# Two fused attention layers on one core: theta and phi split by GpSimd through the staging buffer, a fourth pair buffer, units in new slots, and the turned tile handled later

## The chip, the cores and the metric

The kernel runs on one core of a Trainium2 chip. The metric is the device time of one execution, in microseconds (us). The kernel before took 1897.72 us, the median of three runs (1893.85 to 1898.34). One execution was profiled; it took 1896.21 us, of which the trace spans 1894.4 us.

Engines are named as in the profile: PE is TensorE, DVE is VectorE, ACT is ScalarE, POOL is GpSimd, SP is SyncE, which here only issues transfers.

## The reference: what is computed

The input `x` has 32 images of 128 channels by 32x32 pixels. Each image goes through two attention layers over its 1024 pixels.

```python
# layer 0 (D = 64)
t = conv1x1(x, W_theta, b_theta); p = conv1x1(x, W_phi, b_phi)
f = softmax(einsum('ndq,ndk->nqk', t, p) / sqrt(D), axis=-1)
x = x + conv1x1(einsum('nqk,nck->ncq', f, x), W_fuse, b_fuse)
# layer 1
h = group_norm(x, gn_w, gn_b)
q, k, v = (conv1x1(h, w, b) for w, b in ((q_w, q_b), (k_w, k_b), (v_w, v_b)))
attn = softmax(einsum('bic,bcj->bij', q, k) * C ** -0.5, axis=-1)
y = x + conv1x1(einsum('bcj,bij->bci', v, attn), p_w, p_b)
```

## The kernel before

**Tiles and slots.** The scores of a layer are 1024x1024, cut into eight tiles of 128 queries by 1024 keys. One iteration of the loop has 16 slots: slots 0 to 7 are the tiles of layer 0 of one image, slots 8 to 15 those of layer 1 of the image before it. Every engine has its own program that runs over the slots (`body`), and the order in it is written out by hand; the engines meet through semaphores only. The loop runs over the 32 images; head and tail iterations do a part of it.

**What PE does in slot s:** the scores of tile s (L429), one small product called a unit (L491), the transposes of the tile before if that one is "turned" (L458), and a quarter of the value product of the group that began six slots or more ago (L467). A group is four tiles: 0 to 3, 4 to 7, 8 to 11 and 12 to 15. Its value product begins in slot 6, 10, 14 and 2 (of the next iteration) and takes four slots. Its first quarter waits for the transfers of the group, for the low half of the turned tile (`s_tlo`), for the values' split (`s_split`) and for the product before to have been taken out of its bank (`s_taken`).

**How a tile gets its exponentials turned.** After the scores, DVE takes the row maximum (L723), ACT the exponential (L622), and the result is kept as two 16-bit halves, hi and lo, that have to be transposed. Tiles 1 and 2 of a group ("crossed") have their hi half made by ACT in `pair` (L647) and their lo half by DVE (L740); tile 0 ("copied") goes to `e_copied`, with its hi half from ACT (L645) and its lo half from POOL (L875). The halves of these three are then transposed by a DMA from `pair` to `et` (L350), one 128x2048 transfer per tile. `pair` has three places, one for each position in a group, so a tile's hi half waits until the transfer of the same position one group earlier has landed (L643). Tile 3 ("turned") is transposed by PE (L464), then ACT writes its hi half (L632) and DVE its lo half (L734).

**SP's queue** holds all transfers, in program order. In each group it issues: the denominators' reciprocals to DRAM (`rden_dram`, L363), then, when they have landed, the same as a broadcast row back to all partitions (`rden_row`, L374), then the three transposes. Between them stand the next image's load (`xs`, L385, slot 1), the stores of the result (L395) and the copies of phi (L405). An instruction of this queue that waits holds up all that follow.

**Units.** `UNITS` (L50) gives the unit of each slot: group norm (`gn1`, `gn2`), values (`v`, `w`), keys, queries, theta with phi (`tp`), and `mx`, a bound on the values. All use one PSUM bank `m_ps`, so a unit waits until ACT has emptied the bank of the one before (`s_evac`). Values, keys and queries go from the bank to `stage` by ACT, which has two places; POOL splits them into hi and lo (`split_units`, L877). Theta and phi don't use the stage: ACT writes the hi halves (L579, L581) and DVE the lo halves (L810, L814), right from the bank to `theta2` and `phi2`; then one DMA per half of the pixels copies phi to the other 64 partitions (L405).

The scores of slot 0 wait for these copies (`s_phi`, L442).

## Time and profile before

| | |
|---|---|
| median of 3 runs | 1897.72 us |
| profiled execution | 1896.21 us |
| its span | 1894.4 us |
| mean granted clock of PE | 0.991 |
| PE busy | 1715.3 us, 91% |
| DVE and ACT busy | 1445.5 and 1445.6 us, 76% each |
| POOL busy | 1260.9 us, 67% |
| packets in the DMA queue, share of 16 engines | 74.8% |

In the profile's lines, L426 is line 426 of the kernel and `o_ps<-et,v_hi` is what an instruction writes and reads. In a group of instructions there follow the shapes, the count, then the busy time in us and the mean ns of one, then the idle time of the engine before them with what ended it. "SPq" is the sequencer of SP, whose lines are issues of transfers.

### The profile page before, as it was taken

The numbers are of one execution on the slowest core, as the hardware profiler recorded it, in microseconds if no ns is written. First come the engines' busy times: TensorE is split into PE (matmuls) and PEld (weight loads), VectorE is DVE, ScalarE is ACT, GpSimd is POOL, SyncE is SP. The second block draws the span as 40 slices with busy tenths as digits, with TensorE's granted clock in tenths as the row PEclk, the third lists the DMA queues.
The fourth block names the chain that finished last, engine by engine and source line by source line (L and its number), as shares of the span: only waits on it lengthen the run. The fifth ranks groups of instructions, "written<-read, shape, count | busy, mean of one in ns | idle before, by whom it ended". The sixth has DMA issues, their size and how long they took to land.

```text
span 1894.4 us, 34418 instructions
## 1 busy us (share of the span) xinstructions
PE 1715.3 (91%) x8970; PEld 1103.0 (58%) x8970; DVE 1445.5 (76%) x1669; ACT 1445.6 (76%) x2152; POOL 1260.9 (67%) x1321
## 2 busy tenths in 40 slices
PE   3799999999999999999999999999999999999986
PEld 2455565656566665556665566665656565556553
DVE  4577778788778777778787778788778877878754
ACT  3587778778778777878787878777878777878754
POOL 2467766667776667776666776666776666776653
PEclk9799999999999999999999999999999999999999
DMA  2587787877787777878877878877878777778764
GB/s 53 115 141 149 158 169 148 160 157 151 162 164 159 158 159 147 164 155 161 161 155 148 165 154 163 165 147 156 164 150 166 162 146 160 163 147 166 149 134 95
DMA packets 860086, 286.33 MB, mean 151 GB/s; under 512 B 822305, under 2 KB 823201, under 8 KB 860065
## 3 DMA queue, kind: packets, MB, share of 16 engines
q1 hardware_dynamic: 860064, 286.08, 74.8%
q8 instruction: 9, 0.15, 0.0%
q14 instruction: 13, 0.10, 0.0%
HBM read 50.86 MB, written 17.04 MB: 36 GB/s over the span
## 4 chain that ended last, share of the span: by engine, by line
issue 25%; DVE 17%; ACT 14%; DMA 13%; PE 11%; POOL 10%; SPq 7%; DVEq 1%; POOLq 0%; ACTq 0%
DMA et<-pair 9%; SPq L350 6%; DVE neg_max L723 6%; PE o_ps L426 6%; ACT s_ps L622 4%; DMA rden_dram<-rden 3%; ACT pair L647 3%; PE s_ps L426 3%; DVE pair L740 2%; DVE phi L814 2%; PE s_ps L464 2%; POOL y_sb L974 2%; DVE x L777 2%; DVE x_max L800 2%; ACT et L632 2%
## 5 line engine op out<-in xcount | busy, mean ns | idle before, releaser
L426 PE MATMUL o_ps<-et,v_hi 128*128 128x512 f16 x2048 | 696.9, 382 | 39.9 <-DVE x L777 27.3
L723 DVE TENSOR_REDUCE neg_max<-s_ps 128x1 f32<-128x1024 f32 x512 | 624.5, 1220 | 62.7 <-PE s_ps L426 52.2
L740 DVE SCALAR_TENSOR_TENSOR pair<-s_ps,pair 128x1024 f16<-128x1024 f32 x256 | 312.3, 1220 | 105.6 <-ACT pair L647 104.6
L426 PE MATMUL o_ps<-et,v_lo 128*128 128x512 f16 x1024 | 390.0, 381 | 0.0
L426 PEld LDWEIGHTS o_ps<-et,v_hi 128*128 128x128 f16 x2048 | 202.7, 99 | 283.6 <-issue 92.5
L426 PE MATMUL s_ps<-phi,theta 128*128 128x512 f32 x1024 | 330.8, 446 | 9.2 <-ACT e_copied L622 4.5
L622 ACT ACTIVATE s_ps<-s_ps,neg_max 128x1024 f32<-128x1024 f32 x256 | 277.2, 1083 | 60.4 <-DVE neg_max L723 59.7
L875 POOL TENSOR_TENSOR pair<-e_copied,pair 128x1024 f16<-128x1024 f32 x128 | 274.2, 2142 | 27.5 <-ACT pair L645 27.5
L964 POOL TENSOR_TENSOR x<-x,xr 128x512 f32<-128x512 f32 x64 | 81.1, 1267 | 283.4 <-DVE x L777 283.4
L734 DVE SCALAR_TENSOR_TENSOR et<-s_ps,et 128x1024 f16<-128x1024 f32 x128 | 156.7, 1224 | 146.4 <-ACT et L632 146.4
L647 ACT ACTIVATE pair<-s_ps 128x1024 f16<-128x1024 f32 x256 | 261.9, 1023 | 8.1
L426 PE MATMUL s_ps<-k_hi,q_hi 128*128 128x512 f32 x512 | 246.3, 481 | 7.9 <-POOL q_lo L875 2.3
L645 ACT ACTIVATE pair<-e_copied 128x1024 f16<-128x1024 f32 x128 | 135.3, 1057 | 150.5 <-DMA et<-pair 145.6
L426 PEld LDWEIGHTS s_ps<-phi,theta 128*128 128x128 f32 x1024 | 195.9, 192 | 70.4 <-ACT e_copied L622 6.2
L426 PE MATMUL s_ps<-k_hi,q_lo 128*128 128x512 f32 x512 | 202.1, 395 | 0.0
L426 PE MATMUL s_ps<-k_lo,q_hi 128*128 128x512 f32 x512 | 201.5, 393 | 0.0
L622 ACT ACTIVATE e<-s_ps,neg_max 128x1024 f32<-128x1024 f32 x128 | 142.5, 1114 | 47.1 <-DVE neg_max L723 45.3
L632 ACT ACTIVATE et<-s_ps 128x1024 f16<-128x1024 f32 x128 | 131.1, 1024 | 58.3 <-PE s_ps L464 56.2
L464 PE MATMUL s_ps<-ident_sb,e 128*128 128x128 f32 x1024 | 138.1, 278 | 32.4 <-ACT e L622 32.4
L875 POOL TENSOR_TENSOR v_lo<-stage,v_hi 128x512 f16<-128x512 f32 x128 | 148.5, 1160 | 10.7
L622 ACT ACTIVATE e_copied<-s_ps,neg_shifted 128x1024 f32<-128x1024 f32 x128 | 143.0, 1117 | 4.2
L464 PEld LDWEIGHTS s_ps<-ident_sb,e 128*128 128x128 f32 x1024 | 109.8, 141 | 61.8 <-ACT e L622 61.8
(131 smaller groups left out, 2885.1 us busy)
## 6 DMA issues: line engine op xcount, KB each, us to landing
rden_row<-rden_dram SPq DMA_DIRECT2D x128, 256.0 KB, 3.8
xs<-in_x SPq DMA_DIRECT2D x32, 512.0 KB, 3.9
phi<-phi SPq DMA_DIRECT2D x64, 256.0 KB, 3.1
out_y<-y_sb SPq DMA_DIRECT2D x64, 256.0 KB, 2.4
et<-pair SPq DMA_TRANSPOSE x384, 4.6
rden_dram<-rden SPq DMA_DIRECT2D x128, 2.0 KB, 1.5
w_f<-in_w_fuse_t SPq DMA_DIRECT2D x1, 64.0 KB, 2.2
ident_sb<-in_ident SPq DMA_DIRECT2D x1, 64.0 KB, 2.1
```

The costliest lines, as they stand in the source:

```text
L350: sp.dma_start_transpose(et[:, t // GROUP % 4, r, :, :], pair[:, r, :, :].rearrange("q a n -> q (a n)")).then_inc(s_pair_t[r], 16)
L426: mm = pe.matmul(out, lhs_t, rhs, start=start and n == 0, stop=stop and n == len(terms) - 1)
L464: mm = pe.transpose(s_ps[:, part(t), kb * P:(kb + 1) * P], e[:, kb * P:(kb + 1) * P], ident[:, :])
L622: nc.scalar.activation(to[:, :], s_ps[:, r, :], ACT.Exp, bias=bias, accum_out=den[:, g, t % GROUP:t % GROUP + 1]).then_inc(s_exp, 1)
L632: nc.scalar.activation(et[:, t // GROUP % 4, TURNED, 0:KB, :], s_ps[:, part(t), :].rearrange("k (b q) -> k b q", b=KB), ACT.Copy, scale=E_ ...
L645: nc.scalar.activation(pair[:, r, 0, :], e_copied[:, :], ACT.Copy).then_inc(s_copied_hi, 1)
L647: nc.scalar.activation(pair[:, r, 0, :], s_ps[:, part(t), :], ACT.Copy, scale=E_SCALE).then_inc(s_pair_hi, 1)
L723: nc.vector.tensor_reduce(neg_max[:, t % 4:t % 4 + 1], s_ps[:, part(t), :], AX.X, ALU.max, negate=True).then_inc(s_max, 1)
L734: nc.vector.scalar_tensor_tensor(out=blocks[:, KB:2 * KB, :], in0=s_ps[:, part(t), :].rearrange("k (b q) -> k b q", b=KB), scalar=E_SCALE, ...
L740: nc.vector.scalar_tensor_tensor(out=pair[:, r, 1, :], in0=s_ps[:, part(t), :], scalar=E_SCALE, in1=pair[:, r, 0, :], op0=ALU.mult, op1=AL ...
L875: nc.gpsimd.tensor_tensor(out, in_, hi, ALU.subtract).then_inc(sem, 1)
L964: nc.gpsimd.tensor_tensor(x1[:, cols], x1[:, cols], xr[:, cols], ALU.add).then_inc(s_x1, 1)
```

## The change

1. **Theta and phi through the stage.** ACT writes the unit `tp` as one 128x512 activation to `stage`. POOL makes hi and lo from it in a new buffer `tp_hl`. Four DMAs per half of the pixels bring them to `phi2` (two times hi and lo) and `theta2` (hi and lo). The four instructions of ACT and DVE per half go.
2. **Two parts of pair.** `PAIRS` is 4; the copied tile uses place 0 and place 3 in turn, so its hi half waits for the transfer of two groups ago.
3. **Units in new slots**, with a new table of stage places and of POOL's lags. `mx` moves from slot 14 to 9, `v0` from 15 to 14, `w0` and `w1` from 8 and 9 to 7 and 11, `q1` from 7 to 8. The copies stand in SP's slots 12 and 14, before in 11 and 13.
4. **The turned tile later.** PE runs the quarter of the value product before the transposes of the slot; ACT runs the exponential before the turned hi half; DVE makes the turned lo half one slot later, in the slot in which it also takes out a value product.
5. The units `tp`, `q`, `k` start with the two terms of the hi half and wait for the lo half before the third. The value product's first quarter waits only for the splits of the first half of the values, the third quarter for the rest.

```diff
-UNITS = {0: "gn1", 1: "gn2", 2: "v1", 4: "k0", 5: "k1", 6: "q0", 7: "q1", 8: "w0", 9: "w1", 10: "tp0", 12: "tp1",
-         14: "mx", 15: "v0"}
+UNITS = {0: "gn1", 1: "gn2", 2: "v1", 4: "k0", 5: "k1", 6: "q0", 7: "w0", 8: "q1", 9: "mx", 10: "tp0", 11: "w1",
+         12: "tp1", 14: "v0"}
-PAIRS = 3
+PAIRS = 4
-PHI_SLOTS = {11: "tp0", 13: "tp1"}
+TP_COPY_SLOTS = {12: "tp0", 14: "tp1"}
+    def place(s):
+        return PAIRS - 1 if s % GROUP == COPIED and s // GROUP % 2 else s % GROUP
...
-            def phi_copies(it, s):
+            def tp_copies(it, s):
...
-                sp.wait_ge(s_tp, before(tp_at, it, unit) + 1)
+                sp.wait_ge(s_split, before(staged_at, it, unit) + 1)
                 sp.sem_inc(s_carrier)
-                sp.dma_start(phi2[0:D, :, cols].bitcast(F32), phi2[D:C, :, cols].bitcast(F32)).then_inc(s_phi, 16)
+                sp.wait_ge(s_scores, before(tile_at, it, PHASE))
+                sp.sem_inc(s_carrier)
+                theta_hl, phi_hl = (tp_hl[half][rows, :, :].bitcast(F32) for rows in (slice(0, D), slice(D, C)))
+                sp.dma_start(phi2[0:D, :, cols].bitcast(F32), phi_hl).then_inc(s_tp_copy[half], 16)
+                sp.dma_start(phi2[D:C, :, cols].bitcast(F32), phi_hl).then_inc(s_tp_copy[half], 16)
+                sp.dma_start(theta2[0:D, cols].bitcast(F32), theta_hl[:, 0, :]).then_inc(s_tp_copy[half], 16)
+                sp.dma_start(theta2[D:C, cols].bitcast(F32), theta_hl[:, 1, :]).then_inc(s_tp_copy[half], 16)
...
                     if s == 0:
-                        pe.wait_ge(s_phi, 16 * before(tp_at, it, 0))
+                        for n in range(2):
+                            pe.wait_ge(s_tp_copy[n], 16 * TP_COPIES * before(mx_at, it, 0))
...
                     unit(it, s)
+                    values(it, s)
                     transposes(it, s)
-                    values(it, s)
...
-                if name[0] == "t":
-                    cols = slice(int(name[-1]) * HALF, (int(name[-1]) + 1) * HALF)
-                    act.wait_ge(s_scores, before(tile_at, it, PHASE))
-                    nc.scalar.activation(theta2[0:D, cols], m_ps[0:D, :], ACT.Identity,
-                                         bias=vec_ready[0:D, 0:1]).then_inc(s_theta, 1)
-                    nc.scalar.activation(phi2[D:C, 0, cols], m_ps[D:C, :], ACT.Identity,
-                                         bias=vec_ready[D:C, 0:1]).then_inc(s_evac, 1)
-                    return
+                elif name[0] == "t":
+                    nc.scalar.activation(to, m_ps[:, :], ACT.Identity, bias=vec_ready[:, 0:1]).then_inc(s_evac, 1)
...
                 for s in range(SLOTS):
+                    exponentials(it, s)
                     turned_hi(it, s)
-                    exponentials(it, s)
...
-            def take_lo(it, s):
-                t = s - 2
+            def turned_lo(it, s):
+                t = s - 3
...
                     take_bounds(it, s)
                     maxima(it, s)
+                    turned_lo(it, s)
                     normalised(it, s)
-                    take_lo(it, s)
-                    take_unit(it, s)
+                    pair_lo(it, s)
                     reciprocals(it, s)
+                    bound_to_scale(it, s)
...
                 pool.wait_ge(s_evac, before(taken_at, it, s) + 1)
-                if name[0] in "qk":
+                if name[0] == "t":
+                    pool.wait_ge(s_tp_copy[half], 16 * TP_COPIES * or_none(before(mx_at, it, s) - 1))
+                    hi, lo = tp_hl[half][:, 0, :], tp_hl[half][:, 1, :]
+                    hi_read = hi.bitcast(F32)
+                elif name[0] in "qk":
```

**SP's queue from slot 11 to slot 15, before.** The transfers in program order, in an iteration of the head in which all of them stand; `et<-pair` are the transposes of tiles 9, 8 and 10 and, at the end, of 13 and 12, `phi<-phi` the copies, `rden` the reciprocals.

```order
L350 DMA_TRANSPOSE et<-pair 128x16x128 [waits pair_ready,value_product_ready]
L350 DMA_TRANSPOSE et<-pair 128x16x128 [waits copied_pair_ready,value_product_ready]
L405 DMA phi<-phi 64x2x512 [waits theta_phi_ready]
L350 DMA_TRANSPOSE et<-pair 128x16x128 [waits pair_ready,value_product_ready]
L405 DMA phi<-phi 64x2x512 [waits theta_phi_ready]
L363 DMA rden_dram<-rden 128x4 [waits rden_ready,rden_row_loaded0]
L374 DMA rden_row<-rden_dram 128x512 [waits rden_in_dram0,value_product_taken]
L350 DMA_TRANSPOSE et<-pair 128x16x128 [waits pair_ready,value_product_ready]
L350 DMA_TRANSPOSE et<-pair 128x16x128 [waits copied_pair_ready,value_product_ready]
```

**The same stretch after.**

```order
L364 DMA_TRANSPOSE et<-pair 128x16x128 [waits pair_ready,value_product_ready]
L424 DMA phi<-tp_hl 64x2x512 [waits unit_split,scores_ready]
L425 DMA phi<-tp_hl 64x2x512
L426 DMA theta<-tp_hl 64x512
L427 DMA theta<-tp_hl 64x512
L378 DMA rden_dram<-rden 128x4 [waits rden_ready,rden_row_loaded0]
L424 DMA phi<-tp_hl 64x2x512 [waits unit_split,scores_ready]
L425 DMA phi<-tp_hl 64x2x512
L426 DMA theta<-tp_hl 64x512
L427 DMA theta<-tp_hl 64x512
L389 DMA rden_row<-rden_dram 128x512 [waits rden_in_dram0,value_product_taken]
L364 DMA_TRANSPOSE et<-pair 128x16x128 [waits pair_ready,value_product_ready]
```

The two copies, one before and one behind the transpose of tile 10 and both ahead of the reciprocals, have become eight: four behind that transpose and four between the reciprocals' way out and their way back, ahead of the transposes of tiles 13 and 12.

**DVE in slots 13 and 14, before.** `neg_max` is the maximum of a tile, `et<-s_ps,et` the turned lo half of tile 11, `x<-o_ps` the value product of tiles 4 to 7 taken out, `rden` its reciprocals' last step.

```order
L733 REGISTER_ALU
L734 SCALAR_TENSOR_TENSOR et<-s_ps,et 128x1024 [waits et_hi_ready]
L809 REGISTER_ALU
L810 SCALAR_TENSOR_TENSOR theta<-m_ps,vec_ready,theta 64x512 [waits theta_hi_ready]
L813 REGISTER_ALU
L814 SCALAR_TENSOR_TENSOR phi<-m_ps,vec_ready,phi 64x512 [waits unit_taken_by_act]
L722 REGISTER_ALU
L723 TENSOR_REDUCE neg_max<-s_ps 128x1 [waits scores_ready]
L777 TENSOR_TENSOR x<-o_ps,rden_row 128x512 [waits h_hi_ready,h_ready,x1_res_ready1,rden_row_loaded1,value_product_ready]
L752 SCALAR_TENSOR_TENSOR den_scaled<-den,v_scale,e_factors 128x4 [waits value_scale_ready1,exp_ready]
L756 ISA [waits den_scaled_ready]
L757 RECIPROCAL rden<-den_scaled 128x4 [waits rden_in_dram0]
```

**The same stretch after.**

```order
L749 REGISTER_ALU
L750 TENSOR_REDUCE neg_max<-s_ps 128x1 [waits scores_ready]
L757 REGISTER_ALU
L758 SCALAR_TENSOR_TENSOR et<-s_ps,et 128x1024 [waits et_hi_ready]
L806 TENSOR_TENSOR x<-o_ps,rden_row 128x512 [waits h_hi_ready,h_ready,x1_res_ready1,rden_row_loaded1,value_product_ready]
L781 SCALAR_TENSOR_TENSOR den_scaled<-den,v_scale,e_factors 128x4 [waits value_scale_ready1,exp_ready]
L785 ISA [waits den_scaled_ready]
L786 RECIPROCAL rden<-den_scaled 128x4 [waits rden_in_dram0]
```

The lo half of tile 11 now stands behind the maximum of tile 13, right ahead of the value product that PE waits for; the four instructions on theta and phi of each iteration are gone.

**PE in slot 0, behind the unit `gn1`, before.** `ident_sb,e` are the transposes of the turned tile 15, `o_ps` a quarter of the value product.

```order
L501 MATMUL m_ps<-mean_var,group_avg_sb 128x2 [waits mean_var_ready]
L462 ISA
L464 MATMUL s_ps<-ident_sb,e 128x128 [waits exp_ready]
L464 MATMUL s_ps<-ident_sb,e 128x128 x7
L426 MATMUL o_ps<-et,v_hi 128x512
L426 MATMUL o_ps<-et,v_lo 128x512
L426 MATMUL o_ps<-et,v_hi 128x512 x2
L426 MATMUL o_ps<-et,v_lo 128x512
L426 MATMUL o_ps<-et,v_hi 128x512
```

**The same stretch after.**

```order
L530 MATMUL m_ps<-mean_var,group_avg_sb 128x2 [waits mean_var_ready]
L511 ISA
L448 MATMUL o_ps<-et,v_hi 128x512 [waits unit_split]
L448 MATMUL o_ps<-et,v_lo 128x512
L448 MATMUL o_ps<-et,v_hi 128x512 x2
L448 MATMUL o_ps<-et,v_lo 128x512
L448 MATMUL o_ps<-et,v_hi 128x512
L485 ISA
L487 MATMUL s_ps<-ident_sb,e 128x128 [waits exp_ready]
L487 MATMUL s_ps<-ident_sb,e 128x128 x7
```

The transposes and the six matmuls of the value product have changed places.

## Rows read from the trace of the kernel before

**Rows 1.** The page: busy time, share of the span and instructions; then the DMA queue.
```profile
PE 1715.3 (91%) x8970; PEld 1103.0 (58%) x8970; DVE 1445.5 (76%) x1669; ACT 1445.6 (76%) x2152; POOL 1260.9 (67%) x1321
...
q1 hardware_dynamic: 860064, 286.08, 74.8%
```

**Rows 2.** Waits of the whole span: total us, times, longest us.
```profile
ACT pair L645 <- DMA et<-pair: 145.6, 83, 3.5
...
PE m_ps L426 <- ACT stage L591: 34.0, 30, 1.6
PE s_ps L464 <- ACT e L622: 32.4, 66, 1.4
...
PE o_ps L426 <- DVE x L777: 27.3, 30, 1.4
```

**Rows 3.** PE's timeline: start us, us, instruction.
```profile
156.25 0.38 PE L426 MATMUL o_ps<-et,v_hi 128*128 128x512 f16 x1
...
949.05 0.38 PE L426 MATMUL o_ps<-et,v_hi 128*128 128x512 f16 x1
...
974.78 0.39 PE L426 MATMUL o_ps<-et,v_hi 128*128 128x512 f16 x1
...
983.82 1.27 PE L426 MATMUL s_ps<-phi,theta 128*128 128x512 f32 x4
...
1006.15 0.38 PE L426 MATMUL o_ps<-et,v_hi 128*128 128x512 f16 x1
...
1741.52 0.38 PE L426 MATMUL o_ps<-et,v_hi 128*128 128x512 f16 x1
```

**Rows 4.** SP's timeline in the same iteration: start us, us of issue.
```profile
979.29 0.35 SPq L363 DMA_DIRECT2D rden_dram<-rden  x1
980.89 0.32 SPq L374 DMA_DIRECT2D rden_row<-rden_dram  x1
981.69 8.21 SPq L350 DMA_TRANSPOSE et<-pair  x3
990.38 0.36 SPq L385 DMA_DIRECT2D xs<-in_x  x1
...
1001.44 2.36 SPq L350 DMA_TRANSPOSE et<-pair  x1
```

**Rows 5.** The transpose issued at 1001.44: issue in ns, and from issue to landing.
```profile
L350 SPq DMA_TRANSPOSE et<-pair x1: 2364/2364/2364, 1001.4 to 1001.4; - x1
...
DMA to landing us min/median/max: 4.5/4.5/4.5
```

**Rows 6.** All copies of phi: issue ns min/median/max; from issue to landing.
```profile
L405 SPq DMA_DIRECT2D phi<-phi x64: 590/622/1195, 15.5 to 1769.6; - x64
...
DMA to landing us min/median/max: 3.0/3.1/5.2
```

**Rows 7.** Windows: us, busy of PE, PEld, DVE, ACT, POOL, clock, DMA share, GB/s.
```profile
978.00:978.50 0.50, 0.00 (x0) 0.00 (x0) 0.50 (x1) 0.50 (x1) 0.00 (x0) 1.00 0.84 180
978.50:979.00 0.50, 0.26 (x2) 0.17 (x3) 0.37 (x4) 0.47 (x3) 0.33 (x1) 1.00 1.00 197
979.00:979.50 0.50, 0.50 (x4) 0.24 (x3) 0.50 (x3) 0.50 (x1) 0.50 (x1) 1.00 0.72 148
979.50:982.00 2.50, 2.50 (x16) 2.00 (x14) 2.34 (x5) 1.84 (x4) 2.50 (x2) 1.00 0.03 1
```

**Rows 8.** Groups of instructions, three of DVE and one of PE (L508 is mx).
```profile
L723 DVE TENSOR_REDUCE neg_max<-s_ps 128x1 f32<-128x1024 f32 x512 | 624.5, 1220 | 62.7 <-PE s_ps L426 52.2 <-issue 8.0
...
L734 DVE SCALAR_TENSOR_TENSOR et<-s_ps,et 128x1024 f16<-128x1024 f32 x128 | 156.7, 1224 | 146.4 <-ACT et L632 146.4
...
L777 DVE TENSOR_TENSOR x<-o_ps,rden_row 128x512 f32<-128x512 f32 x64 | 68.0, 1062 | 33.1 <-PE o_ps L426 32.1
...
L508 PE MATMUL m_ps<-w_f_abs,x_max_row 128*128 128x128 f32 x64 | 12.6, 279 | 2.4 <-ACT phi L581 2.4
```

**Rows 9.** The start of the program, PE's timeline: the first scores.
```profile
34.33 3.78 PE L426 MATMUL s_ps<-phi,theta 128*128 128x512 f32 x8 [3.74 <-DVE bound L687]
```

More of the change, by code:

```diff
@@ L162, in until_part_before, with until_stage_before, last @@
         return value(lambda i: count(kind, 0, (part_before(i, s) or 0) + 1), it)
+    def until_stage_before(it, s):
+        def last(i):
+            g = SLOTS * i + s
+            return next((p for p in range(g - 1, -SLOTS - 1, -1)
+                         if staged_at(p) and STAGE[UNITS[p % SLOTS]] == STAGE[UNITS[s]]), -SLOTS - 1)
+        return value(lambda i: count(staged_at, 0, last(i) + 1), it)
+    def place(s):
+        return PAIRS - 1 if s % GROUP == COPIED and s // GROUP % 2 else s % GROUP
     def same_pair(s):
-        return lambda g: int(tile_at(g) and g % GROUP == s % GROUP)
+        return lambda g: int(tile_at(g) and g % GROUP != TURNED and place(g) == place(s))
     def same_group(s):
@@ L220, in attention_pair @@
         phi2 = sb("phi2", [C, 2, N], F32R)
+        tp_hl = [sb(f"tp_hl{n}", [C, 2, HALF], F32R) for n in range(2)]
         q_hi, q_lo = sb("q_hi", [C, N], F32R), sb("q_lo", [C, N], F32R)
@@ L298, in attention_pair @@
         s_den = sem("den_scaled_ready")
-        s_phi = sem("phi_twice")
+        s_tp_copy = [sem(f"theta_phi_copied{n}") for n in range(2)]
         s_split_hi = sem("unit_split_hi")
@@ L350, in move @@
                 sp.dma_start_transpose(et[:, t // GROUP % 4, r, :, :],
-                                       pair[:, r, :, :].rearrange("q a n -> q (a n)")).then_inc(s_pair_t[r], 16)
+                                       pair[:, place(t), :, :].rearrange("q a n -> q (a n)")).then_inc(
+                                           s_pair_t[place(t)], 16)
             def reciprocals_out(it, s):
@@ L395, in stores @@
                 sp.dma_start(batch(y, it.i - 2)[:, cols], y_sb[:, cols]).then_inc(s_store[half], 16)
-            def phi_copies(it, s):
-                unit = next((u for u, name in UNITS.items() if name == PHI_SLOTS.get(s)), None)
+            def tp_copies(it, s):
+                unit = next((u for u, name in UNITS.items() if name == TP_COPY_SLOTS.get(s)), None)
                 if unit is None or not here(tp_at, it, unit):
@@ L473, in values @@
                 if quarter == 0:
-                    for r in range(PAIRS):
-                        pe.wait_ge(s_pair_t[r], 16 * before(same_pair(r), it, first + GROUP))
+                    for t in range(first, first + TURNED):
+                        pe.wait_ge(s_pair_t[place(t)], 16 * before(same_pair(t), it, first + GROUP))
                     pe.wait_ge(s_tlo, before(turned_at, it, first + GROUP))
+                    if first % SLOTS == 0:
+                        pe.wait_ge(s_split, before(staged_at, it, first))
+                    if first % SLOTS == PHASE:
+                        pe.wait_ge(s_split, before(staged_at, it, first))
+                    pe.wait_ge(s_taken, before(group_at, it, first))
+                if quarter == 2:
                     if first % SLOTS == 0:
@@ L480, in values @@
                         pe.wait_ge(s_split, before(staged_at, it, first + 4))
-                    pe.wait_ge(s_taken, before(group_at, it, first))
                 g = first // GROUP % 4
@@ L639, in pair_hi @@
                     return
-                n, r = before(tile_at, it, t), t % GROUP
+                n, r = before(tile_at, it, t), place(t)
                 act.wait_ge(s_exp, n + 1)
@@ L954, in copied_lo @@
                         pool.wait_ge(s_copied_hi, before(copied_at, it, t) + 1)
-                        rest(pair[:, COPIED, 1, :], e_copied[:, :], pair[:, COPIED, 0, :], s_copied)
+                        rest(pair[:, place(t), 1, :], e_copied[:, :], pair[:, place(t), 0, :], s_copied)
             def outputs(it, s):
```

48 lines of the change are left out of this document (21 added, 27 removed).

## The prediction

> **What bounds the kernel now.** I read the busy table and the DMA queue's line first [rows 1]: PE is busy 91% of the span, and the packets fill 75% of the DMA engines' time. That looks like a kernel bound by PE with 9% to win. So the second view is the list of waits [rows 2]: PE loses 34.0 us before the product of tp0 (30 times, some 1.1 us each), 32.4 us before the transposes of turned tiles, 27.3 us before the value product of slot 14 (30 times, 0.9 us each). ACT waits 145.6 us for transfers of `pair`. The change aims at each of these four.
>
> The third view is the timeline, to see how long an iteration is and what closes it. The value product of slot 6 starts at 156.25 and, 28 iterations later, at 1741.52 [rows 3]: 56.62 us per iteration. I cut an iteration at two points: v6, the start of the value product in slot 6 (949.05, next 1006.15 [rows 3]), and R, where SP issues the reciprocals of slot 14 (979.29 [rows 4]). From v6 to R it is 30.24 us, and so 26.4 us are left on average from R to the next v6 (26.86 in this iteration).
>
> The second part is the one to look at. SP's queue holds, from R: reciprocals out (979.29), their row back (980.89), three transposes (981.69, with an issue of 8.21 us), the image (990.38), reciprocals again, and three more transposes, the last issued at 1001.44 [rows 4]. That one takes 4.5 us to land [rows 5], at 1005.96, and the value product starts 0.2 us later, at 1006.15 [rows 3]. So this half is a chain of transfers on one queue, and PE waits at its end. The list of waits hides it: ACT, held by an earlier transfer of the same chain [rows 2], releases the keys' bank so late that the query product ends at the same moment. A fourth place in `pair` takes away ACT's wait, but not the landing.
>
> **The half from v6 to R, part by part.** It is PE's half. Removed: the wait before tp0, 1.1 us, since the copied tile of this group no longer waits for its place; the waits at two of the four turned tiles, 32.4 / 31 / 2 = 0.5 us; smaller gaps, 0.2 us (estimate). Added: mx comes into this half, two matmuls of 279 ns [rows 8], 0.3 us. It also makes DVE take the bound ahead of the maximum in slot 10, and the turned lo half now stands ahead of the value product that DVE takes out. From the end of the scores of slot 9, DVE needs about 0.6 (mx and the bound), 1.22, 1.22 and 1.06 [rows 8], together 4.1 us with hand-overs; PE comes back to its bank after mx, a quarter, the scores and tp0, some 3.7 us (my sum of its timeline). That adds a wait of about 0.35 us. In slots 2, 6 and 14 the same sum without the bound is 3.6 us against 3.5 to 4.0 us of PE's work, so nothing to 0.1 us. In slot 14, R stands 4.51 us behind the scores of slot 13 (974.78 [rows 3] to 979.29 [rows 4]): the theta and phi work of DVE goes (1.5 us) and the turned lo half (1.22 us) comes, so I take 4.4. Sum: 30.24 - 1.1 - 0.5 - 0.2 + 0.3 + 0.35 - 0.1 = 29.0 us, a gain of 1.2 us; with exact hand-overs it could be 28.5, and 30.0 if DVE is late once more.
>
> The removed instructions of ACT and DVE themselves cost nothing and gain nothing else: both are at 76% [rows 1]. POOL gets two more instructions per half of theta and phi, 64 times 1.9 us, that is 67% to 73%; it has each result some 7 us before PE or SP needs it, apart from tp1, whose copies wait behind the reciprocals anyway. If this cover were gone, the queries' split before slot 8 would be the first to show, with about 1 us of room.
>
> **The half from R to v6.** Before, both copies of phi are issued ahead of R. Now four copies stand between the reciprocals' way out and their way back, and three transposes, the image and three more transposes queue behind them. Their size is 256 + 256 + 128 + 128 = 768 KB. One copy of 256 KB occupies the DMA engines for 0.5 x (0.84 + 1.00 + 0.72) = 1.28 us, from 1.2 us behind its issue on [rows 7]; four take 3.84 us. The first is issued at R + 0.4, so its data run from R + 1.6 to R + 5.4. Before, the engines were idle from 979.5 to 982.0 [rows 7] and the row's data began at R + 2.7. The stretch that follows is full of transfers, so the shift does not get lost: 5.4 - 2.7 = 2.7 us, less what the row's read from DRAM now does under cover (0.3 to 0.5 us) and what iterations with a late reciprocal have to spare. I take 2.2 us.
>
> Bounds of this term: at the least SP's own issue counts, two of 0.62 us [rows 6] and two of about 0.35 [the single issues of rows 4], with gaps 2.1 us, which put the row at R + 2.8 instead of R + 1.6, so 1.2 us. At the most all the 3.84 us are added.
>
> Does PE come later than this chain? The scores of slot 0 wait for all copies. Alone a copy lands 3.1 us behind its issue [rows 6]; the other three add 1.28 + 0.64 + 0.64, so the last lands at R + 0.4 + 5.7. Without a wait PE would begin these scores 7.8 us behind the scores of slot 13 (before 9.04 [rows 3], less mx 0.3 and the wait of 0.9); with R at 4.4 the copies land at 10.5. So PE waits 2.7 us there, every iteration, but this wait lies under the chain: with it PE would reach v6 at R + 26.8, the chain at R + 26.4 + 2.2 = 28.6.
>
> A rule of the Trainium skill bears on this term. Its page "DMA: Bandwidth & Descriptors", section "Anatomy of one DMA — SWDGE (gpsimd) path", gives a transfer about 2.0 us and its bytes at 436 GB/s. That would be 0.6 us of data for 256 KB, where the trace has 1.28 us. By the page the four copies would be through in 1.8 us (an estimate from its figure), and only SP's issue would be left.
>
> **Sum.** 29.0 + 28.6 = 57.6 us per iteration against 56.62, rounded to +0.9 because the small gaps of the first half may all close. It counts 31 times: +28 us. At the start the first scores come at 34.33, behind DVE's bounds on the weights [rows 9]. These wait for a product that PE issues behind theta, phi and mx; with mx first and no DVE work on theta and phi this chain gets some 3.6 us shorter, and the copies still land before it ends. The tail, in which there is no theta or phi, gains about 1 us. Against the profiled execution: 1896.2 + 28 - 4.6 = 1919.6 us. The median of the runs is 1.5 us above that execution; the forecast is 1920 us.
>
> **Rivals.**
> - *The copies cost only their issue.* The shift is 1.2 us, the iteration 29.0 + 27.6 = 56.6, with the small gaps 56.5: 1896.2 - 4 - 5 = 1888 us. For it speaks that transposes have long issues and may have slack; against it that three of them take 8.21 us to issue [rows 4], much longer than four copies, as if the transfers ahead held them. By the Trainium skill's rate (page and section as above) it would come out like this.
> - *The chain of transfers isn't the bound and the gain lands.* This needs a shift under 0.4 us, from where on PE's own path decides: 29.0 + 26.8 - 0.1 = 55.7 us: 1896.2 - 28 - 4.6 = 1863 us. For it: PE is the busiest engine by far. Against it: the 0.2 us between landing and v6.
> - *The copies of tp0 collide too.* They follow the transpose of tile 10. If this lands as late as before, their 3.84 us reach beyond R + 1.6, each 0.1 us beyond is 3 us in the sum; at 0.6 us and a shift that is 2.7 instead of 2.2 the iteration is 58.6 us, and the time 1955 us.
> - *Later halves bind.* DVE comes late with the value product in all four slots by 0.4 us, while the chain of transfers keeps its pace: slots 10 and 14 lie in the first half, which then gets 0.8 us longer, less 0.3 of room in slot 14: 1920 + 31 x 0.5 = 1935 us. It decides from 0.3 us of lateness on; in slots 2 and 6 it lies under the chain.
>
> **Numbers.** Forecast with its own spread (1900 to 1942) 50%, issue only 17%, gain lands 13%, tp0 collides 12%, later halves 8%. The range of 8 in 10 reaches from 1868 to 1948. A difference under 0.3%, 5.7 us, cannot be told from none. Faster takes the gain case, most of the issue case (1888 is 0.5% below) and little else: 0.27. Same: 0.12. Slower: 0.61.
>
> **What the profile after would show.** Right: v6 still 0.2 us behind the landing of the third transpose; R to v6 near 28.6 us and v6 to R near 29.0; PE waiting 2 to 3 us before the scores of slot 0 for the copies; ACT's 145.6 us gone; the DMA share of the busiest stretch up by 3.8 us behind R; a DVE wait of 0.3 us at the value product of slot 10. Wrong: PE with no wait in slot 0, or a v6 that follows a PE instruction directly with the last transpose landed a microsecond earlier; a first half not shorter than 30 us would show that the waits on ACT were replaced by waits on DVE.

## The result, and the profile after

| | before | after |
|---|---|---|
| median | 1897.79 us | 1960.63 us (1959.01 to 1962.98) |
| profiled execution's span | 1894.4 us | 1957.2 us |
| granted clock of PE, mean | 0.991 | 0.958 |
| an iteration, mean of 28 | 56.62 us | 58.75 us |
| v6 to R | 30.24 us | 29.23 us |
| R to v6 | 26.38 us | 29.52 us |

The changed kernel takes 1.0337 times as long, 95% interval 1.0319 to 1.0355. The forecast was 1920 us with a range up to 1948 us: the direction was right, but the loss is 62.8 us against 22.3 forecast, 2.8 times as large. All means over an iteration here and below are over the same 28 iterations as in the prediction, from the first v6 to the 29th; lines of a timeline show a single iteration, and the one at 948.50 is longer than most from R to v6 (30.55 us).

The page after: busy time and the DMA queue, which answer to [rows 1].

```profile
PE 1744.0 (89%) x8970; PEld 1126.5 (58%) x8970; DVE 1323.8 (68%) x1541; ACT 1398.0 (71%) x2088; POOL 1383.6 (71%) x1449
...
q1 hardware_dynamic: 879520, 319.65, 78.6%
```

The work moved as the change says: 128 instructions fewer on DVE, 64 fewer on ACT, 128 more on POOL. But PE is busy 29 us longer with the same 8970 matmuls, so some of them run slower.

The waits after, which answer to [rows 2] (total us, times, longest us):

```profile
PE s_ps L448 <- DMA theta<-tp_hl: 97.4, 31, 4.9
...
PE o_ps L448 <- DMA et<-pair: 28.0, 10, 4.5
PE o_ps L448 <- POOL k_lo L895: 24.8, 16, 2.1
...
PE o_ps L448 <- DVE x L806: 11.1, 31, 0.8
```

ACT's 145.6 us for `pair` are gone, and so are PE's waits before tp0 and before the turned transposes. In their place PE waits 3.1 us in each of 31 iterations for the last copy of theta.

SP's timeline, which answers to [rows 4] (start us, us of issue):

```profile
944.73 0.68 SPq L424 DMA_DIRECT2D phi<-tp_hl  x1
945.46 0.60 SPq L425 DMA_DIRECT2D phi<-tp_hl  x1
946.11 0.79 SPq L426 DMA_DIRECT2D theta<-tp_hl  x1
946.94 1.29 SPq L427 DMA_DIRECT2D theta<-tp_hl  x1
948.50 0.36 SPq L378 DMA_DIRECT2D rden_dram<-rden  x1
949.11 0.62 SPq L424 DMA_DIRECT2D phi<-tp_hl  x1
949.78 0.61 SPq L425 DMA_DIRECT2D phi<-tp_hl  x1
950.44 0.68 SPq L426 DMA_DIRECT2D theta<-tp_hl  x1
951.16 1.26 SPq L427 DMA_DIRECT2D theta<-tp_hl  x1
952.68 0.38 SPq L389 DMA_DIRECT2D rden_row<-rden_dram  x1
953.31 8.36 SPq L364 DMA_TRANSPOSE et<-pair  x3
```

R is at 948.50. The first transpose is issued 4.81 us behind it; before it was 2.40 [rows 4]. And look at what stands ahead of R. On DVE's timeline the reciprocals that R sends out are ready 0.74 us earlier (start us, us):

```profile
947.58 0.18 DVE L786 RECIPROCAL rden<-den_scaled 128x4 f32<-128x4 f32 x1
```

SP was still issuing the copies of tp0. PE's timeline behind R, which answers to [rows 3], with the idle time before a matmul in brackets:

```profile
954.93 2.01 PE L448 MATMUL s_ps<-phi,theta 128*128 128x512 f32 x4 [3.02 <-DMA theta<-tp_hl]
...
979.05 0.58 PE L448 MATMUL o_ps<-et,v_hi 128*128 128x512 f16 x1 [2.69 <-DMA et<-pair]
```

Four matmuls that took 1.27 us before [rows 3] take 2.01 us. Windows of the same stretch (us; busy of PE, PEld, DVE, ACT, POOL; then the granted clock, the DMA share, GB/s):

```profile
951.00:954.90 3.90, 0.91 (x5) 0.20 (x2) 2.37 (x3) 1.42 (x3) 1.50 (x2) 1.00 0.89 212
955.00:958.30 3.30, 3.30 (x10) 2.09 (x11) 1.23 (x1) 0.17 (x1) 0.65 (x3) 0.50 1.12 197
958.50:961.00 2.50, 2.50 (x18) 2.09 (x17) 0.03 (x1) 2.20 (x4) 0.66 (x1) 1.00 0.98 185
```

PE stood still for 3.02 us, and then works at half of the full clock (1.2 instead of 2.4 GHz) for 3.4 us. This happens about the scores of slot 0 in all 28 iterations (in two of them it lasts 6.8 us), and in four of them again at v6; before, in none of them. The Trainium skill ("TensorE: Matmul & The Clock Gate", section "HAM oscillation — how this bites in real kernels") describes this: a wait for a transfer that comes back with each tile makes the array throttle each time. The trace agrees: here it comes back in each of the 28 iterations. I had not weighed this page.

### The profile page after: what moved, and what is told of

Same layout as the page of the kernel before. It is cut to its first block, busy times and chain, and to the rows that moved or that the text cites. A ratio compares the mean times of both kernels' runs of the same rounds, so it can differ in the third digit from the quotient of the medians.

```text
span 1957.2 us, 34651 instructions
## 1 busy us (share of the span) xinstructions
PE 1744.0 (89%) x8970; PEld 1126.5 (58%) x8970; DVE 1323.8 (68%) x1541; ACT 1398.0 (71%) x2088; POOL 1383.6 (71%) x1449
## 4 chain that ended last, share of the span: by engine, by line
PE 37%; SPq 20%; issue 14%; POOL 10%; DMA 9%; DVE 6%; ACT 1%; POOLq 1%; DVEq 0%; ACTq 0%
PE o_ps L448 15%; PE s_ps L448 13%; SPq L364 11%; DMA theta<-tp_hl 6%; PE m_ps L448 5%; PE s_ps L487 4%; SPq L426 2%; DVE neg_max L750 2%; SPq L424 2%; SPq L427 2%; SPq L425 2%; POOL h_lo L895 2%; DMA et<-pair 2%; DVE x L806 2%; DVE pair L769 1%
## 5 line engine op out<-in xcount | busy, mean ns | idle before, releaser
L448 PE MATMUL o_ps<-et,v_hi 128*128 128x512 f16 x2048 | 722.9, 395 | 76.2 <-DMA et<-pair 28.0
L448 PE MATMUL s_ps<-phi,theta 128*128 128x512 f32 x1024 | 338.4, 456 | 104.7 <-DMA theta<-tp_hl 97.4
L448 PEld LDWEIGHTS o_ps<-et,v_hi 128*128 128x128 f16 x2048 | 212.7, 104 | 349.8 <-issue 131.3
L448 PE MATMUL o_ps<-et,v_lo 128*128 128x512 f16 x1024 | 404.7, 395 | 0.0
L448 PEld LDWEIGHTS o_ps<-et,v_lo 128*128 128x128 f16 x1024 | 102.8, 100 | 79.4 <-issue 11.4
L487 PEld LDWEIGHTS s_ps<-ident_sb,e 128*128 128x128 f32 x1024 | 128.1, 148 | 33.0 <-issue 8.3
```

The source lines that it names most:

```text
L448: mm = pe.matmul(out, lhs_t, rhs, start=start and n == 0, stop=stop and n == len(terms) - 1)
L487: mm = pe.transpose(s_ps[:, part(t), kb * P:(kb + 1) * P], e[:, kb * P:(kb + 1) * P], ident[:, :])
```

## The experiments

The ratios are to runs of the kernel before on the same chip, with their 95% intervals.

**The fourth place of `pair` alone.**

```diff
 # the kernel before
-PAIRS = 3
+PAIRS = 4
+def place(s):
+    return PAIRS - 1 if s % GROUP == COPIED and s // GROUP % 2 else s % GROUP
...
-        n, r = before(tile_at, it, t), t % GROUP
+        n, r = before(tile_at, it, t), place(t)
```

> The kernel before with the fourth place of pair alone. Theory (v6 follows the landing of the third transpose, so ACT's wait of 145.6 us is free of charge in slots 5 and 6 and only the 1.1 us before tp0 return): 1896 - 31 x 1.1 = 1862 us, the value product of slot 6 still 0.2 us behind its transpose. Rival (ACT's wait holds the query product and so v6): all of the 4.7 us per iteration that ACT waits can't return, but more than 2 us do: under 1835 us. Rival (the wait before tp0 is replaced by another on DVE or SP): 1885 us or more.

1832.76 us, ratio 0.9679 (0.9663 to 0.9695). By its number this is the first rival's case (under 1835 us), and 29 us better than mine. By its mechanism it is not: v6 to R is 28.50 us, R to v6 26.40 us (before 26.38), and v6 stands 0.09 us behind the landing of the third transpose, in the median as in the mean. So the second half is indeed closed by the transposes, and ACT's wait was worth nothing there. What I had too small is the first half, which gains 1.73 us, not 1.1. The stretch that held the wait before tp0, from the value product of slot 9 to that of slot 10, shrinks from 4.76 to 3.39 us, by more than the idle time of 1.12 us in it, and the one from slot 7 to slot 8 from 4.55 to 4.25. The wait before the turned transposes also shrinks, from 32.4 us [rows 2] to

```profile
PE s_ps L468 <- ACT e L626: 18.4, 29, 1.4
```

but the stretch from slot 10 to slot 14, in which that part of it lay, stays (14.14 and 14.19 us). 2 us more go ahead of the first v6 and 6 us in the tail of the program.

**The place of `pair` and the later halves.**

```diff
 # the kernel before with the fourth place; PE, ACT, DVE
                     unit(it, s)
-                    transposes(it, s)
                     values(it, s)
+                    transposes(it, s)
...
-                    turned_hi(it, s)
                     exponentials(it, s)
+                    turned_hi(it, s)
...
                     maxima(it, s)
+                    turned_lo(it, s)      # t = s - 3, in take_lo it was s - 2
                     normalised(it, s)
```

> The kernel before with the fourth place of pair, and with the turned tile's transposes behind the value product and its halves later; theta and phi and the units stay as they were. Theory (these parts are the gain of the change, the copies its loss): the wait before tp0 (1.1 us) and that before the turned transposes (0.5 us) go, R to v6 stays at 26.4: 1896 - 31 x 1.6 = 1847 us. Rival (DVE, which still has theta's and phi's low halves, is late at the value product with the later lo half, in slot 10 and slot 14 by 0.5 us or more): 1847 + 31 x 1.0 = 1878 us. Rival (in the kernel before the chain of transfers absorbs what PE gains): 1890 us or more.

1834.98 us, ratio 0.9685 (0.9667 to 0.9703), the same as with the fourth place alone. v6 to R falls to 28.02 us, R to v6 is 26.53 us; the 0.35 us per iteration that this wins come back at the ends of the program, where the first v6 stands at 158.3 instead of 154.2 us and the stretch behind the 29th is 4.0 us longer. The rival in which DVE is late falls.

**PE's and ACT's order later, DVE's low half not.**

```diff
 # the kernel before with the fourth place: PE and ACT as above, DVE as before
```

> The kernel before with the fourth place of pair and with PE's turned transposes behind the value product and ACT's turned half behind the exponential, but DVE's turned low half still two slots behind its tile. Theory (the iteration is now bound by PE in v6 to R and by DVE's readiness and the transposes in R to v6; the order of PE moves at most 0.4 us): v6 to R 27.9 to 28.5 us, R to v6 26.4 us, 1825 to 1838 us. Rival (DVE now waits for ACT's later turned half ahead of the next maximum, some 1 us in each of four slots, and PE with it): 1870 us or more.

1972.65 us, ratio 1.0428 (1.0399 to 1.0457): the rival, and more than it said. DVE now stands before the low half until ACT has written the high one; the wait of the whole span was 153.1 us with the fourth place alone and is

```profile
DVE et L738 <- ACT et L636: 327.9, 128, 2.9
```

Both halves of the iteration grow (30.42 and 28.83 us). Part of it is again the clock, which falls shortly ahead of R or behind it in most of the iterations (the mean of the profiled execution is 0.963). The three moves of the edit before belong together.

**The four copies, put into the fast kernel.**

```diff
 # the kernel before with the fourth place
-PHI_SLOTS = {11: "tp0", 13: "tp1"}
+PHI_SLOTS = {12: "tp0", 14: "tp1"}
...
                 sp.dma_start(phi2[0:D, :, cols].bitcast(F32), phi2[D:C, :, cols].bitcast(F32)).then_inc(s_phi, 16)
+                sp.dma_start(spare[half][D:C, :, :].bitcast(F32), phi2[D:C, :, cols].bitcast(F32)).then_inc(s_phi, 16)
+                sp.dma_start(spare[half][0:D, 0, :].bitcast(F32), theta2[0:D, cols].bitcast(F32)).then_inc(s_phi, 16)
+                sp.dma_start(spare[half][0:D, 1, :].bitcast(F32), theta2[D:C, cols].bitcast(F32)).then_inc(s_phi, 16)
```

> The kernel before with the fourth place of pair and, behind the reciprocals' way out where the changed kernel has its copies, phi's copy and three more of the changed kernel's sizes into spare tiles that nobody reads (PE waits for all four). Theta and phi are still taken by ACT and DVE, and the units stand where they did. Theory (the four copies are the whole loss: 1.5 us per iteration by their issue, 1.6 us by their data in R to v6, 0.7 us by the clock in the first half): R to v6 29.0 to 29.7 us, v6 to R 28.5 to 29.3 us, 1838 + 31 x 3.8 = 1956 us, and 1934 us where the clock holds. Rival (the theta and phi path over POOL or the new unit slots cost the time, the copies only coincide): under 1880 us.

1919.05 us, ratio 1.0101 (1.0081 to 1.0121), 78 us of span above the kernel without them. R to v6 is 28.78 us, 2.38 more, and the first transpose is issued 4.77 us behind R. v6 to R stays at 28.60. The expectation of 1956 us was too high in two terms. The copies move v6 by 2.38 us, not by 3.1, so that even the 1934 us for a clock that holds were too many. And the 0.7 us for the clock are not there: PE waits only 1.73 us before the scores of slot 0 here,

```profile
PE s_ps L434 <- DMA spare<-theta: 53.7, 31, 2.7
```

and the clock stays full in 26 of 28 iterations. So the copies are the largest part of the loss, and 41 us remain to be found in the other edits. The opposite run, the changed kernel with one copy per half instead of four (forecast 1851 us, rival at least 1900), gave no time, so the other edits without the three more copies were never measured.

**The copies' issue without their data.**

```diff
 # the changed kernel, in the loop
-                sp.dma_start(phi2[0:D, :, cols].bitcast(F32), phi_hl).then_inc(s_tp_copy[half], 16)
+                sp.dma_start(phi2[0:D, :, few].bitcast(F32), phi_hl[:, :, 0:16]).then_inc(s_tp_copy[half], 16)
 # ... and so for the other three
```

> The changed kernel with its four copies per half still issued at the same places, but in the loop each carries 16 of 512 columns (so stale theta and phi are used). Theory now (the copies cost SP's time to issue them, some 3.5 us behind R in the trace after, and their data only add PE's wait at the scores of slot 0 and the half clock behind it): the reciprocals' row is still issued 3.5 to 4.2 us behind R, PE's wait before the scores of slot 0 shrinks from 3.0 to under 1 us, and R to v6 is 28.0 to 28.8 us: 1957 - 31 x 1.1 = 1923 us. Rival (an issue is long because the data of the transfers ahead hold the queue): the issues shrink to 0.3 us each, R to v6 falls to about 26.6 us, 1957 - 31 x 2.9 = 1867 us. Rival (neither matters, the new slots do): within 6 us of 1960.

This kernel leaves out most of theta and phi, so its result is not the reference's; apart from the width of the copies its instructions are those of the changed kernel. 1897.24 us, ratio 1.0024 (1.0013 to 1.0035); R to v6 27.93 us, v6 to R 28.56 us. SP's timeline:

```profile
1201.20 0.60 SPq L429 DMA_DIRECT2D theta<-tp_hl  x1
1202.14 0.35 SPq L378 DMA_DIRECT2D rden_dram<-rden  x1
1202.74 0.62 SPq L426 DMA_DIRECT2D phi<-tp_hl  x1
1203.40 0.61 SPq L427 DMA_DIRECT2D phi<-tp_hl  x1
1204.07 0.60 SPq L428 DMA_DIRECT2D theta<-tp_hl  x1
1204.70 0.60 SPq L429 DMA_DIRECT2D theta<-tp_hl  x1
1205.56 0.37 SPq L389 DMA_DIRECT2D rden_row<-rden_dram  x1
```

A copy costs SP 0.60 to 0.62 us to issue, with 4 or 8 KB as with 256 KB; only the last two of a row of four get longer with data (0.68 and 1.26 us in the trace after). By itself the issue moves v6 by 27.93 - 26.38 = 1.55 us. In 15 of the 28 iterations the clock fell between R and v6, at another place than in the changed kernel (the value product of slot 2); over the other 13 the mean is 27.63 us, so 1.25 us are the issue's own. The rest of what the copies cost, 1.1 us of 2.4, is their data. Neither one-sided theory holds. The kernel comes out 26 us below my number, since R is no longer late (below) and the clock falls neither behind the scores of slot 0 nor at v6.

**tp1's copies behind the row.**

```diff
-TP_COPY_SLOTS = {12: "tp0", 14: "tp1"}
+TP_COPY_SLOTS = {12: "tp0", 15: "tp1"}
...
 # SP, slot 15
                     reciprocals_in(it, s)
+                    if s == 15:
+                        tp_copies(it, s)
                     transposes(it, s)
```

> The changed kernel with tp1's four copies issued behind the reciprocals' row instead of ahead of it (nothing else moves; three transposes follow them as before). Theory (the first transpose of the chain is what the copies hold back, by SP's issue and by data, whichever side of the row they stand on): the row is issued 1.6 us behind R, but the transposes come as late, v6 stays; the scores of slot 0 get their copies some 1.6 us later, so PE waits longer there: 1960 to 1985 us. Rival (the late row is what costs, through POOL's value scale and DVE's take-out of the product): R to v6 back under 28 us, 1957 - 31 x 1.5 = 1910 us.

2086.73 us, ratio 1.098 (1.0953 to 1.1007), far beyond both numbers. The row goes out early and gains nothing; the copies, no longer issued in the 2 us in which SP waits for the reciprocals to land anyway, push the first transpose from R + 4.8 to R + 6.6, and the last copy lands at R + 9.9 instead of R + 6.3. PE's wait doubles,

```profile
PE s_ps L451 <- DMA theta<-tp_hl: 208.6, 31, 7.8
```

the clock falls every time, and v6 comes 4.0 us later although the first transpose comes only 1.8 us later. The additional 2.2 us went through PE: the reciprocals of the next group go out at R + 20.48, when the third transpose has long landed (R + 16.93).

**All copies on ACT's queue.**

```diff
-                    tp_copies(it, s)       # SP
...
+                    tp_copies(it, s)       # ACT, behind take_unit and inputs_hi
```

> The changed kernel with all eight copies issued on ACT's queue (behind its take of the unit in slots 12 and 14), none on SP's. Theory (SP's issue is 1.5 us of the loss in R to v6, data 1.6 us): the row is back at 1.6 to 1.9 us behind R, R to v6 falls from 29.5 to 28.0 us, ACT pays 8 issues of 0.6 us per iteration, part of it where DVE waits for it: 1957 - 31 x 1.5 + 31 x 0.5 = 1926 us, 1911 us where ACT has the room. Rival (the data are all that counts, the issue is hidden behind them): 1955 us or more. Rival (the two queues' transfers overlap and the data vanish too): 1870 us.

2234.35 us, ratio 1.1734 (1.1692 to 1.1775); no theory gave this. ACT's timeline shows why (ACTq is its sequencer):

```profile
1690.17 0.62 ACTq L669 DMA_DIRECT2D phi<-tp_hl  x1
1690.83 1.41 ACTq L670 DMA_DIRECT2D phi<-tp_hl  x1
1692.27 1.62 ACTq L671 DMA_DIRECT2D theta<-tp_hl  x1
1693.92 1.96 ACTq L672 DMA_DIRECT2D theta<-tp_hl  x1
1696.07 0.30 ACT L628 ACTIVATE neg_shifted<-neg_max,log_e 128x1 f32<-128x1 f32 x1 [5.29 <-issue]
```

The four issues take 5.6 us instead of the 3.4 of tp0's copies on SP, while three transposes are being issued on SP, and those take 11.68 us instead of 8.36. ACT stands still behind its own issues for 5.29 us; the copies of tp1 wait for ACT's turn and PE for them. Of the two queues SP's was the better one: SP has nothing to compute.

**PE kept at work in its wait.**

```diff
 # the changed kernel, PE, ahead of the wait for the copies in slot 0
+                        if it.like > 0:
+                            pe.wait_ge(s_evac, before(taken_at, it, 0))
+                            product(m_ps[:, 0:2 * C], FILL * [(      # FILL is 16
+                                w_hl["tp"][:, 0, :], w_hl["tp"][:, :, :].rearrange("p a c -> p (a c)"))])
```

> The changed kernel with 16 matmuls of 256 columns more, between the value product of slot 15 and the scores of slot 0, into the unit's bank, which nobody reads before it is written again. By the pace of 512-column matmuls in the trace (some 0.23 us) they fill 1.8 us (estimate) of PE's wait of 3.0 us. Theory (the wait lowers PE's granted clock to half for 3.4 us, and that costs 0.7 us in v6 to R and 0.7 to 1.1 us in R to v6; it is why R to v6 is 29.5 us and not 28.8 us as in the kernel with four places of pair and four copies): the copies still land 6.3 us behind R, the granted clock stays at full speed, v6 to R 28.5, R to v6 28.6 to 28.9 us: 1957 - 31 x 1.4 = 1914 us. Rival (the clock's fall is a bystander; the order of units and the later lo halves make DVE late in slots 0 to 2): 1950 to 1960 us. Rival (the added matmuls delay the scores): over 1960 us.

1932.28 us, ratio 1.0204 (1.0179 to 1.0229). Sixteen useless matmuls make the changed kernel 1.3% faster. PE's timeline, and the 3.3 us behind the scores, to be set beside the window at 955.00:

```profile
1234.96 2.25 PE L449 MATMUL m_ps<-w_tp_hl 128*128 128x256 f32 x16
1238.42 1.17 PE L449 MATMUL s_ps<-phi,theta 128*128 128x512 f32 x4 [1.20 <-DMA theta<-tp_hl]
```

```profile
1238.50:1241.80 3.30, 3.30 (x21) 2.45 (x22) 1.23 (x1) 0.98 (x3) 1.51 (x3) 1.00 1.13 210
```

The copies land at R + 6.30 as after (6.28), but between R and v6 the clock stays full in 25 of 28 iterations, the scores take 1.17 us, and R to v6 falls from 29.52 to 28.87 us. v6 to R stays at 29.20, against the expectation: the 0.7 us there do not come from this fall of the clock. (At v6 it still falls in three iterations.)

**The units in their slots of before.**

```diff
 # the changed kernel
-UNITS = {0: "gn1", 1: "gn2", 2: "v1", 4: "k0", 5: "k1", 6: "q0", 7: "w0", 8: "q1", 9: "mx", 10: "tp0", 11: "w1",
-         12: "tp1", 14: "v0"}
+UNITS = {0: "gn1", 1: "gn2", 2: "v1", 4: "k0", 5: "k1", 6: "q0", 7: "q1", 8: "w0", 9: "w1", 10: "tp0", 12: "tp1",
+         14: "mx", 15: "v0"}
```

> The changed kernel with the units in their slots of before (queries' second product in 7, values' in 8 and 9, mx in 14, v0 in 15); theta and phi still go over ACT and POOL and four copies per half. Theory (with mx in slot 14 PE comes to the scores of slot 0 some 0.4 to 1.0 us later, so it waits 2 to 2.6 us instead of 3.0 us; the copies' shift stays): R to v6 29.0 to 29.5 us, mx moves 0.3 us between the halves; if the clock no longer falls 1957 - 31 x 1.2 = 1920 us, if it does 1945 to 1957 us. Rival (the new slots are what costs the changed kernel its 41 us against the kernel with four places and four copies, clock or no clock): 1916 us with R to v6 at 28.8 us. Rival (the new slots are a gain by themselves): over 1965 us.

1918.57 us, ratio 1.0146 (1.0122 to 1.017). R to v6 28.86 us, v6 to R 28.41 us. PE waits less for the copies,

```profile
PE s_ps L448 <- DMA theta<-tp_hl: 58.4, 31, 3.5
```

and the clock falls between R and v6 in 6 of 28 iterations. The time is at the theory's number (1920 us) and at the rival's (1916 us); by halves it is both. R to v6 loses the 0.66 us of the clock. v6 to R loses 0.82 us, which filling the wait did not return (29.20 us). Over the iterations in which the clock doesn't fall at v6 it is 28.36 us here and 29.03 us in the changed kernel, and this difference belongs to the new slots. It does not come from mx: from the value product of slot 8 to that of slot 10 it is 7.63 us here, with w1 in slot 9, and 7.64 us in the changed kernel, with mx and DVE's wait in its place. From slot 10 to slot 12 it is 6.40 and 6.74 us (w1 now lies here, in slot 11), and from slot 12 to slot 14 7.25 and 7.56 us. In slot 14 the old units have only mx, and PE waits 0.59 us for DVE there; the new ones have v0, which fills this wait and takes more. v0 came from slot 15, where it shortened PE's wait for the copies (1.81 us here, 3.07 us in the changed kernel, on the mean of the 28).

**The image's load out of the chain.**

```diff
 # the kernel before with the fourth place
-XS_SLOT = 1
+XS_SLOT = 4
```

> The kernel before with the fourth place of pair and the load of the next image moved from slot 1 to slot 4, behind the three transposes that v6 waits for. Theory (R to v6 is a chain of transfers on one queue, so what is taken out of its middle returns): 0.36 to 0.68 us of issue and up to 1.3 us of data per iteration, R to v6 24.8 to 26.0 us, 1838 - 31 x 0.8 = 1813 us. Rival (PE's own path is as long as the chain by now): 1830 to 1840 us. Rival (the image comes too late for DVE's maximum in slot 7): over 1845 us.

1877.44 us, ratio 0.9874 (0.9855 to 0.9894), slower than without this edit. R to v6 falls as expected, but by 0.42 us only (25.98), and v6 to R grows from 28.50 to 30.18 us, 1.5 of it up to the next value product, for which PE now waits for transposes. No rival named this. The load now stands right ahead of that group's transposes, but that its data hold them is argued and not shown.

## Why the prediction was wrong, and where it was right

The runs make a path from the kernel before to the changed one, by the spans of the profiled executions:

| step | span, us | change | ratio to before |
|---|---|---|---|
| before | 1894.4 | | 1 |
| fourth place of `pair` | 1838.1 | -56 | 0.9679 |
| and four copies per half | 1915.8 | +78 | 1.0101 |
| and theta and phi over POOL, later halves | 1917.1 | +1 | 1.0146 |
| and units in new slots, wait filled | 1938.2 | +21 | 1.0204 |
| wait not filled: the changed kernel | 1957.2 | +19 | 1.0337 |

By the ratios the third step is 0.5% and the last two are 0.6 and 1.3%; the executions profiled for the fourth place and for the filled wait are 7 and 8 us above their medians. In us of the kernel before, the ratios say -61, +80, +9, +11 and +25, so the split of the last 40 us between slots and clock is known to some 10 us.

**What closes the iteration: right.** In all 28 iterations of the changed kernel v6 follows the landing of the third transpose by 0.29 to 0.32 us. (The list of waits puts half of these to POOL's `k_lo`. That ends anywhere from 1.51 us ahead of v6 to 0.14 us behind its start, so it isn't what ends the wait.) The fourth place of `pair` moved the first half and left the second at 26.40 us.

**The copies' shift: right in size, wrong in make-up.** I took 2.2 us; the runs show 2.38 (fast kernel with four copies) and 2.49 (filled wait). Theta's copies cost SP 0.6 us like phi's, not the 0.35 I took from single small issues, but the issue alone moves v6 by 1.25 us (my bound was 1.2), since part of it lies in the 1.4 us in which the reciprocals are on their way anyway. The data add 1.1 us. By the Trainium skill's rate ("DMA: Bandwidth & Descriptors", section "Anatomy of one DMA — SWDGE (gpsimd) path"), which is for transfers that GpSimd issues and not SP, only the issue would have been left, and the run with 16 columns shows what that is: 1.1 us per iteration less, besides the clock. Its fixed part comes near: a copy of 8 KB lands 1.8 us behind its issue. Its rate does not: with 256 KB it is 3.1 us [rows 6].

**The failed step: "this wait lies under the chain".** PE's wait was foreseen, at its place and in its size (2.7 us forecast, 3.02 measured), and the copies land where I said (R + 6.1, measured R + 6.3). I costed it at nothing because PE would reach v6 at R + 26.8, and the chain at R + 28.6. Two things were missing. PE's wait lowers its clock, so that what follows takes longer than in the trace of before. And the chain does not run on SP's queue alone: ahead of its last three transposes SP issues the reciprocals of the next group, which DVE makes from what PE delivers behind this wait, and then their row, 0.22 us behind their landing in every iteration. SP's lines for these two, in an iteration of the changed kernel with R at 890.59 and in one of the filled wait with R at 882.64:

```profile
906.95 0.32 SPq L378 DMA_DIRECT2D rden_dram<-rden  x1
908.56 0.32 SPq L389 DMA_DIRECT2D rden_row<-rden_dram  x1
```

```profile
897.44 0.33 SPq L379 DMA_DIRECT2D rden_dram<-rden  x1
900.17 0.32 SPq L390 DMA_DIRECT2D rden_row<-rden_dram  x1
```

On the mean these reciprocals go out at R + 13.17 before, at R + 14.99 with the wait filled and at R + 16.53 in the changed kernel. In the first two they land 2.45 and 2.51 us behind the landing of the third transpose that SP issues behind R, and likewise in the runs with the fourth place alone, with the four copies, with narrow copies and with the old units (2.40 to 2.53): the transfers decide. In the changed kernel that transpose has landed at R + 15.15, before they are issued; they land 3.06 us behind it, and PE decides. So the row goes out at R + 18.44 instead of 17.93, the last transpose ahead of v6 lands at 29.23 instead of 28.58, and R to v6 is 29.52 instead of 28.87 us. A margin of 1.8 us at the end of a half is no cover for a delay at its beginning, if the chain is fed from what lies between.

**A second term that was missing: R itself.** I counted the copies behind R, and held against those of tp0 only their data (the rival with 12%). Their issue is what mattered. SP is busy with them until 948.23, and R stands 0.82 us behind the ready reciprocals on the mean, before 0.26: 0.56 us per iteration in v6 to R. With narrow copies it is 0.27.

**v6 to R: 29.0 forecast, 29.23 measured, with errors on both sides.** The wait before tp0 and the one before the transposes were to give 1.6 us; the place of `pair` by itself gives 1.73. For the new slots I counted 0.65 us, 0.3 for mx and 0.35 for DVE's wait. The wait came: 11.1 us over 31 times, 0.36 us each, at the product of slot 10. But I misread where mx stands. In the trace of before it already lies in this half, 28.4 us behind v6 and so 1.8 us ahead of R, and in slot 9 it only takes the place of w1 (7.64 us against 7.63). What the new slots add is w1 in slot 11 and v0 in slot 14, which I had not counted: 14.30 against 13.64 us from slot 10 to slot 14. That these 0.66 us equal my 0.65 is luck. Against the forecast stand further the 0.56 us of R, and 0.2 us for the four iterations in which the clock fell at v6. What makes up for most of that is a gain that I had costed at nothing: from slot 10 to slot 14 it is 13.64 us with the old units, against 14.19 in the kernel with the fourth place and 14.04 with the later halves. DVE has less to do there without theta and phi, but the copies' slots and the start of the units differ too, and no run parts them; this cause isn't shown.

**The sum.** Forecast +0.98 us per iteration, rounded down to +0.9; measured +2.13. The difference is 0.65 (clock behind the scores), 0.2 (clock at v6), 0.56 (R) and 0.3 (the copies' shift), less some 0.5 of gains beyond those I counted; the last term is what is left over, not a measurement. I also rounded towards the smaller loss without a row for it. The head came as forecast (the first scores 4.2 us earlier, the first value product 4.0, with 3.6 forecast), but the gain is lost before the first v6, which is 2.0 us later.

**The rivals.** "Issue only" named half of the copies' shift, 1.25 of 2.4 us. "Gain lands" did not come, and its reason is refuted: with the fourth place alone the gain lands, while v6 still follows its transpose. "tp0 collides" named the right copies and the wrong cost: it is their issue ahead of R, 0.56 us per iteration, and its 1955 us lie near the result for other reasons. "Later halves bind" did not come: these halves cost nothing while DVE moves with PE and ACT.

Both kernels are beaten by the one with the fourth place of `pair` alone: 1832.76 us against 1960.63 and 1897.79 us.

## What to carry to other kernels

When a change moves a wait to the engine that does the matmuls, ask what feeds the chain behind that wait, and look at the granted clock: here a wait of 3 us halved it for the next 3.4 us, and 16 useless matmuls in the wait made the kernel 1.3% faster. Count every issue on the queue that orders the chain, also those ahead of the cut point, at the price of a transfer of the same kind in the trace. And try the parts alone: here one small part carried a gain of 3.2%, and the rest of the change turned it into a loss of 3.4%.

## What the hardware showed unexpectedly

- Issuing a copy from one part of the on-chip memory to another holds SP for 0.60 to 0.62 us whether it carries 4 or 256 KB; the fourth in a row, with the data of the others under way, takes 1.26 to 1.29 us.
- Around a wait without a matmul of 3.1 us on the mean PE's granted clock fell to half in 28 of 28 iterations, for 3.4 us in 26 of them and 6.8 us in two. With mean waits of 1.7 and 1.8 us at the same place it did so in 2 and 6 of 28, with 1.2 us left of the wait in 3. But in the run with narrow copies a mean wait of 1.9 us, ahead of the value product of slot 2, had it fall in 15 of 28: the length of the wait alone doesn't settle it.
- Copies issued on ACT's queue beside transposes on SP's made both slower, in the rows shown: 5.6 instead of 3.4 us for the four issues, 11.7 instead of 8.4 us for the three.
